# Moving the last additions of a token group behind chunk 2 of the next group on VectorE

## The reference

```python
def _quantum_transform(hidden, theta, w_real, w_imag):
    imag = w_imag * jnp.sin(theta + hidden * 0.1)
    quantum_phase = jnp.cos(theta) * w_real + jnp.sin(theta) * w_imag
    return hidden + quantum_phase * imag * 0.1

hidden = jnp.einsum('bsd,df->bsf', x, W1) + b1
q = _quantum_transform(hidden, quantum_phases, quantum_weights_real, quantum_weights_imag)
act = jax.nn.relu(q)
ffn = jnp.einsum('bsf,fd->bsd', act, W2) + b2

xn = _layernorm(x, axis=-1)
x = x + attn(xn) + ffn(xn)      # attn: causal softmax attention, then @ Wo
```

## Time and profile before

| what | us |
|---|---|
| median of 2 timed runs | 1248.31 (1247.38 to 1249.23) |
| the profiled execution | 1225.3 |
| its span, slowest core (core 2) | 1223.6 |
| span of the other cores | 1211.2 to 1219.4 |
| TensorE matmul busy | 1066.3 (87%) |
| VectorE busy | 453.0 (37%) |
| ScalarE busy | 592.9 (48%) |

### The profile page before, as it was taken

One profiled execution on the slowest core, in us unless ns is written; L12 is line 12 of the kernel. 1 busy time (PEld: TensorE's weight loads), 2 busy tenths in 40 slices (PEclk: granted clock), 3 DMA queues, 4 the chain that ended last, 5 costly groups with the idle time before them and its releaser, 6 DMA issues.

```text
span 1223.6 us, 23744 instructions; the slowest of 8 cores (1211.2 to 1223.6 us)
## 1 busy us (share of the span) xinstructions
PE 1066.3 (87%) x7810; PEld 728.6 (60%) x7936; DVE 453.0 (37%) x1007; ACT 592.9 (48%) x1285; POOL 37.1 (3%) x48
## 2 busy tenths in 40 slices
PE   0756486659999999999999999999999999999997
PEld 0644374446666656665666566656666666666665
DVE  2726562623333333333333333333333333333333
ACT  2865385525444544454545454544454544444444
POOL 1220032000000000000000000000000000000000
PEclk9978796979999999999999999999999999999999
DMA  7859687950202030203020202020202020202000
GB/s 157 248 103 170 162 269 120 170 128 1 87 1 87 1 87 1 87 1 87 1 87 2 87 1 87 2 86 2 87 1 87 1 87 1 87 1 87 23 31 36
DMA packets 47416, 87.13 MB, mean 71 GB/s; under 512 B 7106, under 2 KB 23490, under 8 KB 46274
## 3 DMA queue, kind: packets, MB, share of 16 engines
q1 hardware_dynamic: 36226, 59.39, 16.3%
q0 software_dynamic: 11072, 26.22, 11.8%
HBM read 78.25 MB, written 25.17 MB: 85 GB/s over the span
## 4 chain that ended last, share of the span: by engine, by line
PE 72%; issue 2%; DVEq 2%; DVE 2%; ACT 1%; ACTq 0%
PE psOut L833 36%; PE psW L807 36%; DVEq L753 2%; DVE probs L755 1%; ACT rb_sb L780 1%; DVE u_sb L732 1%; DVE out_sb L755 0%; PE psOut L823 0%; DVEq L760 0%; DVEq L731 0%; DVEq L752 0%; DVEq L729 0%; ACTq L779 0%; ACTq L777 0%; ACT ss_sb L772 0%
## 5 line engine op out<-in xcount | busy, mean ns | idle before, releaser
L807 PE MATMUL psW<-xn_r,W_sb 128*128 128x256 bf16 x4096 | 538.9, 275 | 9.7 <-PEq L452 9.7
L833 PE MATMUL psOut<-W_sb,rb_sb 128*128 128x512 bf16 x1936 | 514.8, 382 | 16.4 <-ACT rb_sb L780 10.3
L807 PEld LDWEIGHTS psW<-xn_r,W_sb 128*128 128x128 bf16 x4096 | 404.9, 99 | 170.4 <-issue 13.8
L732 DVE SCALAR_TENSOR_TENSOR u_sb<-ss_sb,Rp_sb,psW 128x256 f32<-128x256 bf16 x512 | 244.4, 480 | 593.5 <-ACT ss_sb L772 580.5
L772 ACT ACTIVATE ss_sb<-psW,phb_sb 128x256 bf16<-128x256 f32 x512 | 242.4, 474 | 444.2 <-PE psW L807 444.2
L833 PEld LDWEIGHTS psOut<-W_sb,rb_sb 128*128 128x128 bf16 x2048 | 200.6, 98 | 150.4 <-issue 19.5
L780 ACT ACTIVATE rb_sb<-u_sb,b_sb 128x256 bf16<-128x256 f32 x511 | 254.5, 498 | 57.2 <-DVE u_sb L732 55.1
L608 DVE CAST pT_big<-psT 128x512 bf16<-128x512 f32 (+2 forms) x80 | 49.0, 612 | 34.4 <-PE psT L556 30.1
L556 PE MATMUL psT<-diag_li,xn_rg 128*128 128x128 bf16 x272 | 27.2, 236 | 32.4 <-DVE pT_big L608 17.0
L436 PE MATMUL psTx<-diag_li,probs 128*128 128x128 bf16 x176 | 15.0, 234 | 45.6 <-DVE diag_li L324 43.3
L556 PEld LDWEIGHTS psT<-diag_li,xn_rg 128*128 128x128 bf16 x272 | 18.0, 103 | 41.6 <-issue 41.6
(11 more groups left out here) (91 smaller groups left out, 425.4 us busy)
## 6 DMA issues: line engine op xcount, KB each, us to landing
x_sb<-x SPq DMA_DIRECT2D x52, 512.0 KB, 6.3
W_sb<-w POOLq DMA_DIRECT2D x8, 2048.0 KB, 42.6
xn_scr<-xn_rg POOLq DMA_DIRECT2D x32, 256.0 KB, 4.8
xn_r<-xn_scr SPq DMA_DIRECT2D x16, 512.0 KB, 8.0
out<-out_sb SPq DMA_DIRECT2D x32, 256.0 KB, 3.3
out<-probs SPq DMA_DIRECT2D x32, 256.0 KB, 6.1
xn_r<-x SPq DMA_DIRECT2D x12, 512.0 KB, 6.8
Q_fm<-b2rep SPq DMA_DIRECT2D x1, 512.0 KB, 4.5
```

Of the source, the lines that this page charges most:

```text
L732: su2.inc(v.scalar_tensor_tensor(u2_sb[ci % 2][:], ss_sb[ci % 2][:], Rp_sb[:, c:c + 1], psW1[slot][:], ALU.mult, ALU.add))
L807: ins = t.matmul(psW1[slot][:], W1_sb[:, k * DFF + c * 128: k * DFF + (c + 1) * 128], xn_r3[g % 2][:, k * R3:(k + 1) * R3], start=(k == 0) ...
L833: ins = t.matmul(psOut[tt][:, h * 512:(h + 1) * 512], rb_sb[cw % 3][:, tt * 128:(tt + 1) * 128], W2_sb[:, cc * D + h * 512: cc * D + (h + ...
```

## The change

The four additions of psOut, with their waits and drains, become a function fin_adds(v, gp) for group gp. VectorE calls it for the group before when it has issued the scalar_tensor_tensor of chunk 2 (c == 2, for every group but the first), and once more for the last group behind the loop. The call at the end of every group is gone. Operands, waits and the order of the increments stay the same; no other engine's program changes.

```diff
+                def fin_adds(v, gp):
+                    for tt in range(2):
+                        j = 2 * gp + tt
+                        v.wait_ge(sw2.h, sw2_b + NCF * (gp + 1))
+                        v.drain()
+                        for hh in range(2):
+                            soadd.inc(v.tensor_tensor(
+                                out_sb2[j % 2][:, hh * 512:(hh + 1) * 512],
+                                psOut[tt][:, hh * 512:(hh + 1) * 512],
+                                out_sb2[j % 2][:, hh * 512:(hh + 1) * 512],
+                                ALU.add))
+
...
                             su2.inc(v.scalar_tensor_tensor(
                                 u2_sb[ci % 2][:], ss_sb[ci % 2][:], Rp_sb[:, c:c + 1],
                                 psW1[slot][:], ALU.mult, ALU.add))
+                            if c == 2 and g >= 1:
+                                fin_adds(v, g - 1)
                             if c == 16:
...
-                        for tt in range(2):
-                            j = 2 * g + tt
-                            v.wait_ge(sw2.h, sw2_b + NCF * (g + 1))
-                            v.drain()
-                            for hh in range(2):
-                                soadd.inc(v.tensor_tensor(
-                                    out_sb2[j % 2][:, hh * 512:(hh + 1) * 512],
-                                    psOut[tt][:, hh * 512:(hh + 1) * 512],
-                                    out_sb2[j % 2][:, hh * 512:(hh + 1) * 512],
-                                    ALU.add))
+                    fin_adds(v, NRG - 1)
```

## The result

The changed kernel takes 1249.08 us (median of 9 runs, 1247.79 to 1250.69). Against runs of the kernel before on the same chip the ratio is 1.0216, with a 95% interval of 1.0203 to 1.0230: it is slower by 2.2%, or 26.4 us on the 1222.7 us that the ratio implies for the kernel before. Of the eight runs of the kernel before, four took 1221.94 to 1224.28 us, and the ratio goes by these; the other four, the two ahead of the prediction (1247.38 and 1249.23 us) among them, were in a slower state that a kernel here falls into at times, and took 1240.27 to 1251.60 us.

What follows compares the result with a forecast made beforehand. TensorE was taken to set the time, with waits where one 256-token group gives way to the next. +18.2 us of wait and +8.5 of clock, less 0.7, gave +26 on 1248.3: 1274.3 us, range 1263 to 1284.

Steps and rivals of the forecast that it cites:

- The move: Whole kernel: the change makes it 26 us slower, +2.1%; chance 0.61.
- What goes: Group boundary: chunks 0 and 1 no longer queue behind the additions on VectorE, saving 0.83 us each, 12.5 us in all.
- What comes: Group boundary: additions wait behind chunk 2 on VectorE and start 2.04 us later; net +1.21 us each, +18.2 us in all.
- The clock: TensorE at boundaries: longer wait makes the clock fall at all 15, not 7, at 1.35 us each; +8.5 us.
- The 0.7 us taken off for the first boundaries: First boundaries: 0.7 us subtracted from +26.7 us, since they come before the pattern is steady.
- The other queues: SP's stores and the loads behind them go 2.04 us later, at no cost; ScalarE waits in the gap anyway.
- Only the wait: Rival at the boundaries: the clock falls no more often than now; +15.8 us, 1264 us; chance 0.13.
- Every fall at full price: Rival: clock falls at all 15 boundaries, always after work has resumed; +31.6 us, 1280 us; chance 0.08.
- A deeper fall: Rival: clock drops mid-wait and a second 3.4 us at 0.50 follows; 1300 us, or 1283 at a third; chance 0.09.
- Nothing moves: Rival at the boundaries: the 0.83 us gain and the delay cancel; 1245 to 1252 us; chance 0.05.
- Faster: Rival: additions block nothing; 1224 to 1236 us if the first starts less than 0.83 us later than now; chance 0.04.

Runs made afterwards that it cites:

- run 22: Not a run label: in "had run 22 us faster" it is a verb and a time, about the profiled execution of the kernel before, 1225.3 us.
- the filled kernel: Changed kernel plus eight idle 128x512 matmuls on TensorE before the first Wo matmul at each of 15 boundaries; 1230.09 us, ratio 1.0061 to the kernel before.
- 0.6 us more: Changed kernel plus one unused 128x512 addition on VectorE ahead of the four at each boundary; 1259.06 us, ratio 1.0283 to the kernel before.
- the last two: Call behind chunk 0 with chunk 0's products each behind its Wo matmul: 1187.81 us, 0.9701; the same with chunk 3's hidden features ahead: 1176.86 us, 0.9612.

## Why the prediction was right or wrong

**The time: wrong.** 1274.3 us was forecast, with 1263 to 1284 as the range, and 1249.08 came. The step that failed is the last of the sum, "I know no reason why the difference should change": the sum was first made on the span, 1223.6 + 26 = 1249.6 (the span came out at 1249.0), and then moved by 24.7 us onto the median of two timed runs, 1248.31. That base was not the kernel's: the four runs that the ratio goes by took 1221.94 to 1224.28 us. (That the span was met to 0.6 us is in part luck: the slowest core's span lies between 1246.1 and 1249.0 us from run to run.) The sign was in the table ahead of it: the profiled execution took 1225.3 us, 1.8% less than the lower of the two timed runs, so this program had run 22 us faster than in either of them. A range that took both for possible bases, 1225 and 1248, would have held the result; the one given treated the base as certain and spent its width on the change. Between kernels run side by side the move is 26.4 us.

**The move: right**, +26 us forecast, +2.16% measured where +2.1% was given.

**What goes, 0.83 us a boundary: right.** TensorE's wait for the Relu fell to 0.2 us in all, and the kernel with the call behind chunk 0, which has this part alone and no falls, lies at 58.05 us: 58.88 - 0.83.

**What comes, 2.04 us: right.** The additions start 0.09 us behind chunk 2's L744. Net 1.21 us was forecast, and the filled kernel gives 60.08 - 58.88 = 1.20.

**The clock, 1.35 us a boundary at all 15: right in size, in part by luck.** All 15 boundaries of the slowest core fell, 14 on four others. The price is 61.44 - 60.08 = 1.36 us in the steady state, but it is no constant: it is 61.76 - 60.08 = 1.68 us at the first boundaries, as at 7 of 15 before. The prediction took the fall to come at a fixed distance from the start of the wait. The traces show it at a fixed distance from the last fall, 61.44 us, with the boundaries coming later against it until it lay inside the wait. That this gives nearly the same price as the assumption was not foreseen. The 0.7 us taken off for the first boundaries has the wrong sign on the slowest core, whose first distances are the longest. The Trainium skill's page "TensorE: Matmul & The Clock Gate", section "HAM oscillation — how this bites in real kernels", has the penalty as half of the throttled time in every round. "Every round" now holds, but for the first boundary of four cores. The half holds at the first boundaries (3.4 us at 0.50 cost 1.68) and not in the steady state, where it cost 1.36, since part of it lay in the wait, which would have been idle anyway. The whole price, 1280 us in the prediction's terms, was too much by 0.3 us a boundary in the steady state.

**The other queues at no cost: right.** No wait for a store or a load stands on TensorE's list in this block.

**The rivals.** Only the wait: it needed the falls to stay at 7, and there were 15; with nearly all falls filled away the changed kernel is at 1.0061, not 1.0216. Every fall at full price: held at the first three distances of the slowest core and no longer. A deeper fall: did not come with this wait, but did with 0.6 us more. Nothing moves: its 1245 to 1252 us hold the measured 1249.08, and its mechanism is refuted all the same, since the delay did not cancel the gain but outweighed it by 1.20 us a boundary; its time came out only because it stood on the same base, 1248.3, which was some 26 us too high. Faster: its point of decision was named rightly, the first addition less than 0.83 us later than before; behind chunk 1 it is 0.3 us later, and that kernel is faster by 1.6%.

## What to carry to other kernels

Before an instruction is moved down an in-order queue, ask what the one ahead of it waits for. Behind work whose input is ready, the move is free; behind work that needs the very last thing the bottleneck engine made before it stops, the whole latency of that chain is added to its wait. And when timed runs and the profiled execution of the same kernel differ by more than the runs' own scatter, the base is uncertain by that much, and a forecast of a time has to say so.

## What the runs showed of the hardware

- The clock's price can be bought back with work that does nothing: 7 idle matmuls of 0.22 us at each boundary made the kernel before 0.9% faster, 8 the changed one 1.5%.
- The stretch at 0.50 was 3.4 us long in every fall at the boundaries of the two kernels, whatever the wait. With a wait 0.6 us longer some lasted 6.8 us.
- In the changed kernel the falls of every core are 61.44 us apart, and the distance of boundaries settles at that value, from above on the slowest core and from 60.08 us on cores 0, 3, 4 and 5. So in the steady state a little more or less wait does not change the distance; with 0.6 us more it settled there too on three cores. Why the falls keep this distance was not tried.
- One boundary in each of several kernels is about 0.35 us later than the rest, at the same place of the program on all eight cores: the 12th in the changed kernel and the first filled one, the 4th in the kernel with the call behind chunk 0 and in the last two. With the extra addition it is the 13th, by 1.2 us. In the changed kernel it is the boundary at 1001.40 of core 6, whose L744 starts that much late, after a ScalarE instruction:

```profile
1000.70 0.48 DVE L744 SCALAR_TENSOR_TENSOR u_sb<-ss_sb,Rp_sb,psW 128x256 f32<-128x256 bf16 x1 [1.61 <-ACT rb_sb L785]
```

  Its cause stays open; no run was made for it.
